# Products of the identity between the first turns, and new orders for the first and last turns of a pipelined kernel

## The reference

```python
down = relu(x @ Wd_b.T + bd); x = x + down @ Wu_b.T + bu          # weights generated per sequence
x = ((layernorm(x) * weight + bias) + tanh(cond)) * weight + bias # layer 1
h = layernorm(x) * g1 + b1; q, k, v = split(h @ W_qkv.T + b_qkv)  # 16 heads of 16
x = x + (softmax(q @ k.T / 4) @ v) @ W_o.T * a1 ...
h = layernorm(x) * g2 + b2; x = x + gelu(h @ W_f1.T + b_f1) @ W_f2.T * a2 ...
val, gate = split(rmsnorm(x) * scale @ up_w.T)
y = act_quant(val * gelu(gate)) @ weight_quant(down_w).T + x
```

## Time and profile before

| | us |
|---|---|
| median of 3 runs | 934.63 (933.69 to 936.41) |
| the profiled execution | 935.74 |
| its span | 933.9 |
| PE busy | 843.1 (90%) |
| DVE busy | 565.4 (61%) |
| ACT busy | 510.9 (55%) |
| POOL busy | 231.2 (25%) |

### The profile page before, as it was taken

The page is one execution under the profiler, slowest core; times in us unless marked ns, Lnnn a source line. Parts: engine busy times, 40 slices in busy tenths (PEclk is TensorE's granted clock), DMA queues, the critical chain, the costliest instruction groups (busy, mean ns, idle before and its releaser), DMA issues.

```text
span 933.9 us, 15916 instructions
## 1 busy us (share of the span) xinstructions
PE 843.1 (90%) x5852; PEld 633.5 (68%) x5852; DVE 565.4 (61%) x1063; ACT 510.9 (55%) x796; POOL 231.2 (25%) x333
## 2 busy tenths in 40 slices
PE   6642577999999999999999999999999999999977
PEld 4101355687777778787878787878777777776665
DVE  1212586575757667575858585858485867656424
ACT  1101444565565657574748575656666574756542
POOL 1001204150405041323232231405050514130310
PEclk9855777999999999999999999999999999999998
DMA  9997643423161433324151515151424132320000
GB/s 344 365 366 252 248 138 124 148 80 122 62 203 38 135 97 114 120 78 156 47 187 47 188 47 188 46 173 61 154 76 142 65 127 80 104 80 25 24 12 12
DMA packets 58477, 118.48 MB, mean 127 GB/s; under 512 B 6336, under 2 KB 15936, under 8 KB 55696
## 3 DMA queue, kind: packets, MB, share of 16 engines
q1 hardware_dynamic: 58400, 117.48, 36.6%
HBM read 82.77 MB, written 34.16 MB: 125 GB/s over the span
## 4 chain that ended last, share of the span: by engine, by line
PE 74%; issue 9%; DMA 7%; DVE 4%; ACT 2%; SPq 2%; POOL 2%; POOLq 0%; DVEq 0%; ACTq 0%
PE bank L486 30%; PE bank L692 11%; PE pair_s L653 6%; PE pair_s L618 5%; PE pair_t L639 5%; PE pair_t L486 4%; DMA hyp<-in_hyper 3%; PE bank L737 3%; PE bank L664 3%; PE bank L567 2%; PE bank L729 1%; PE bank L561 1%; DVE oq L1145 1%; DMA wc<-in_cols 1%; PE bank L574 1%
## 5 line engine op out<-in xcount | busy, mean ns | idle before, releaser
L851 ACT ACTIVATE Pr<-pair_t 128x1024 f32<-128x1024 f32 x128 | 131.3, 1026 | 125.2 <-PE pair_t L639 121.5
L1121 DVE TENSOR_REDUCE nmax<-pair_s 128x4 f32<-128x1024 f32 x128 | 155.8, 1217 | 34.5 <-PE pair_s L618 33.9
L692 PE MATMUL bank<-wf,G 128*128 128x256 f32 x512 | 123.0, 387 | 0.1
L486 PE MATMUL bank<-wup_hi,hD_hi 128*128 128x512 f32 x256 | 109.4, 427 | 4.8 <-POOL hD_lo L1316 4.1
L1344 POOL TENSOR_TENSOR x<-x,xcr 128x512 f32<-128x512 f32 x16 | 20.5, 1281 | 358.1 <-DVE x L1179 358.1
L692 PEld LDWEIGHTS bank<-wf,G 128*128 128x128 f32 x512 | 93.3, 190 | 15.5 <-issue 0.2
L486 PE MATMUL bank<-wup_lo,hD_hi 128*128 128x512 f32 x256 | 102.0, 398 | 0.0
L486 PE MATMUL bank<-wup_hi,hD_lo 128*128 128x512 f32 x256 | 101.9, 398 | 0.0
L618 PE MATMUL pair_s<-Kp,Qp 64*128 64x256 f32 x512 | 66.1, 337 | 21.7 <-DVE nmax L1121 13.0
L895 ACT ACTIVATE gl<-bank,rsD 128x512 f32<-128x512 f32 x64 | 44.1, 689 | 63.6 <-PE bank L486 63.4
L1189 DVE SCALAR_TENSOR_TENSOR hd<-bank,rsD,gl 128x512 f32<-128x512 f32 x64 | 47.9, 748 | 46.2 <-PE bank L486 34.7
(11 more groups left out here) (177 smaller groups left out, 1879.5 us busy)
## 6 DMA issues: line engine op xcount, KB each, us to landing
hyp<-in_hyper SPq DMA_DIRECT2D x16, 1024.0 KB, 10.2
Qp<-qk_scratch SPq DMA_DIRECT2D x64, 256.0 KB, 3.7
Kp<-qk_scratch SPq DMA_DIRECT2D x64, 256.0 KB, 3.6
qk_scratch<-q_hi SPq DMA_DIRECT2D x16, 512.0 KB, 2.8
qk_scratch<-k_hi SPq DMA_DIRECT2D x16, 512.0 KB, 4.0
tC<-rows_scratch SPq DMA_DIRECT2D x16, 384.0 KB, 3.6
cur_scratch<-gen SPq DMA_DIRECT2D x16, 256.0 KB, 10.1
xT_t<-in_xT SPq DMA_DIRECT2D x16, 256.0 KB, 4.2
```

Of the source, the lines that this page charges most:

```text
L486: mm = pe.matmul(dst, l, r, start=first and i == 0, stop=last and i == 2)
L692: mm = pe.matmul(bank[5][:, r * D:(r + 1) * D], G[:, k, r * P:(r + 1) * P], wf2[:, k, :], start=k == 0, stop=k == FT - 1)
L851: act.activation(Pr[:, p % 4, :, :].rearrange("p a n -> p (a n)"), pair_t[:, :, :].rearrange("p a n -> p (a n)"), ACT.Exp, scale=DH ** -0. ...
L1121: dve.tensor_reduce(nmax[:, n % 2, :, p % GP, :], pair_s[:, :, :].rearrange("p a (r n) -> p a r n", r=RT), AX.X, ALU.max, negate=True).the ...
```

## The change

Seven entries W.warm come into PE's table, one in turn 0 between W.qkv and A.q, one between B.o3 of turn 1 and A.up of turn 2, five in turn 2 after B.s0. Each runs keep_clock: three products of the identity by 192 columns into bank 6, whose result nobody reads. In turn 0, ACT's A.down comes ahead of its W.qkv, and DVE's W.qkv comes behind A.cur; ACT splits wf between A.ht and A.q. The tables of turns 0 to 4 are changed for all engines, and in the tail DVE's turn 14 (A.lng and D.u1 swapped) and PE's turn 15 (C.g1 ahead of B.t4, A.v ahead of B.t5). SP waits before each store of q or k that all head loads of the sequence before have landed. The diff, cut:

```diff
     "SP": """
-        0: A.load A.qs A.ks A.ql0 A.kl0 A.ql1 A.ql2 A.ql3 A.kl1 A.kl2 W.late A.kl3 1: B.m0 A.load B.m1 A.qs A.ql0 A.ks A.ql1 2: C.tc 1: A.ql2 A.kl0
-        A.kl1 A.ql3 A.kl2 A.kl3 2: B.m0 A.load B.m1 A.qs A.ql0 A.ql1 A.ql2 A.ks A.kl0 A.ql3 3: C.tc 2: A.kl1 A.kl2 3: A.load B.m0 2: A.kl3 3: B.m1
-        A.qs A.ql0 A.ks A.kl0 D.y0 A.ql1 A.ql2 4: C.tc 3: D.y1 A.ql3 A.kl1 A.kl2 4: B.m0 A.load 3: A.kl3 4: A.qs A.ql0 A.ks A.ql1 B.m1 A.ql2 A.kl0
-        A.kl1 A.ql3 A.kl2 D.y0 D.y1 A.kl3""",
+        0: A.load A.qs A.ks A.ql0 A.ql1 A.kl0 W.late 2: C.tc 0: A.ql2 A.kl1 A.kl2 A.ql3 A.kl3 1: A.load B.m0 B.m1 A.qs A.ql0 A.ql1 A.ks A.ql2 A.kl0
+        A.kl1 A.ql3 A.kl2 A.kl3 2: A.load B.m0 A.qs A.ql0 A.ks B.m1 A.ql1 A.ql2 A.kl0 A.ql3 A.kl1 A.kl2 3: C.tc B.m0 2: A.kl3 3: A.load B.m1 A.qs A.ks
+        A.ql0 D.y0 A.kl0 4: C.tc 3: A.ql1 A.ql2 A.kl1 A.kl2 A.ql3 A.kl3 4: B.m0 A.load 3: D.y1 4: A.qs A.ql0 A.ks A.ql1 A.ql2 A.kl0 A.kl1 B.m1 A.ql3
+        A.kl2 D.y0 A.kl3 D.y1""",
     "PE": """
-        0: A.down A.up W.qkv A.ht A.q A.k A.v 1: A.down A.up B.s0 B.s1 B.s2 B.s3 A.ht B.m0 B.s4 B.s5 B.t0 B.s6 B.t1 B.s7 B.t2 A.q B.m1 A.k B.t3 B.o0
-        B.t4 B.o1 B.t5 A.v B.t6 2: A.down 1: B.t7 B.o2 B.o3 2: A.up C.proj B.s0 B.s1 C.ht B.s2 W.fa W.abs B.s3 C.f0 B.m0 C.f1 B.s4 A.ht C.f2 B.s5 C.f3
...
-        B.o0 4: A.down 3: B.o1 B.t4 C.g0 B.t5 D.y0 D.qt1 B.t6 C.g1 C.g2 B.t7 C.g3 B.o2 B.o3 D.y1 4: B.s0 A.up 3: C.xt 4: C.proj B.s1 D.u0 B.s2 D.u1
-        C.ht B.s3 D.u2 C.f0 C.f1 B.m0 C.f2 B.s4 A.ht C.f3 D.u3 B.s5 A.q B.t0 B.s6 A.k B.s7 D.qt0 A.v B.t1 B.m1 D.y0 B.t2 C.g0 B.t3 C.g1 B.t4 B.o0 B.o1
...
+        0: A.down A.up A.ht W.qkv W.warm A.q A.k A.v 1: A.down A.up B.s0 B.s1 B.s2 B.s3 B.m0 B.s4 A.ht B.s5 B.t0 B.s6 B.t1 B.s7 A.q A.k B.m1 B.t2 B.o0
+        B.t3 B.t4 B.o1 B.t5 A.v B.t6 B.o2 B.t7 2: A.down 1: B.o3 W.warm 2: A.up C.proj B.s0 W.warm B.s1 W.warm W.fa B.s2 W.warm C.ht W.warm W.warm
+        B.s3 C.f0 B.m0 C.f1 B.s4 C.f2 B.s5 A.ht C.f3 B.s6 B.t0 W.abs B.s7 A.q B.m1 B.t1 A.k A.v B.t2 B.o0 C.g0 B.t3 C.g1 B.t4 B.o1 B.t5 C.g2 B.t6 C.g3
+        B.t7 3: A.down 2: B.o2 B.o3 C.xt W.up 3: A.up B.s0 C.proj D.u0 B.s1 D.u1 B.s2 C.ht D.u2 B.s3 C.f0 B.m0 C.f1 B.s4 C.f2 C.f3 A.ht B.s5 B.t0 D.u3
+        B.s6 A.q B.s7 B.t1 A.k B.t2 A.v B.m1 B.t3 B.o0 C.g0 B.t4 B.o1 C.g1 D.qt0 B.t5 C.g2 B.t6 C.g3 B.t7 D.y0 D.qt1 B.o2 B.o3 4: A.down 3: D.y1 4:
+        B.s0 3: C.xt 4: C.proj B.s1 A.up D.u0 B.s2 D.u1 C.ht D.u2 B.s3 C.f0 C.f1 B.m0 C.f2 C.f3 A.ht B.s4 D.u3 B.s5 A.q A.k B.t0 B.s6 A.v C.g0 B.s7
+        B.t1 C.g1 B.t2 B.m1 B.o0 B.t3 C.g2 B.t4 D.qt0 B.o1 B.t5 C.g3 B.t6 D.y0 D.qt1 B.t7 B.o2 D.y1 B.o3 C.xt""",
     "ACT": """
-        0: W.qkv A.down A.lnb A.ht A.q W.fa A.k A.v 1: A.down W.up A.lnb A.ht B.t0 B.t1 A.q B.t2 B.t3 B.t4 A.k B.t5 A.v B.t6 B.t7 2: A.down C.lnb C.ht
-        A.lnb C.f0 C.f1 A.ht C.f2 C.f3 B.t0 A.q B.t1 A.k B.t2 B.t3 B.t4 A.v B.t5 B.t6 B.t7 C.xt 3: A.down D.u0 C.lnb D.u1 C.ht D.u2 C.f0 A.lnb C.f1
...
+        0: A.down W.qkv A.lnb A.ht W.fa A.q A.k A.v 1: A.down A.lnb A.ht B.t0 W.up B.t1 A.q B.t2 B.t3 B.t4 B.t5 A.k B.t6 A.v B.t7 2: A.down C.lnb C.ht
+        C.f0 A.lnb C.f1 C.f2 A.ht C.f3 B.t0 A.q B.t1 A.k B.t2 B.t3 B.t4 B.t5 A.v B.t6 B.t7 3: A.down 2: C.xt 3: D.u0 C.lnb D.u1 C.ht D.u2 A.lnb C.f0
...
     "DVE": """
-        0: W.qkv A.up A.lna A.lng A.ln A.q A.cur A.k 1: A.up A.lna B.s0 A.lng B.s1 A.ln B.s2 B.s3 B.p0 B.m0 B.s4 B.s5 A.cur B.s6 B.s7 B.p1 W.fa B.m1
-        W.up A.q A.k B.o1 W.abs B.o3 2: A.up C.proj C.ln B.s0 B.s1 A.lna A.lng B.s2 A.ln B.s3 B.p0 B.m0 B.s4 B.s5 A.cur B.s6 B.s7 B.p1 A.q A.k B.m1
...
+        0: A.up A.lna A.lng A.ln A.cur W.qkv A.q A.k 1: A.up B.s0 A.lna B.s1 A.lng B.s2 A.ln B.s3 B.p0 B.m0 B.s4 B.s5 B.s6 B.s7 A.cur B.p1 W.fa B.m1
+        A.q W.up B.o1 W.abs A.k B.o3 2: A.up C.proj B.s0 C.ln B.s1 B.s2 A.lna A.lng A.ln B.s3 B.p0 B.m0 B.s4 B.s5 B.s6 B.s7 B.p1 A.q A.cur B.m1 A.k
...
     "PE": """
...
-        D.u1 C.ht B.s3 D.u2 C.f0 B.m0 C.f1 C.f2 B.s4 A.ht C.f3 B.s5 B.t0 D.u3 B.s6 A.q D.qt0 B.s7 B.t1 A.k D.y0 B.m1 B.t2 B.o0 B.t3 C.g0 B.t4 C.g1
-        B.o1 B.t5 A.v B.t6 D.qt1 C.g2 C.g3 B.t7 D.y1 B.o2 B.o3 C.xt 16: B.s0 C.proj B.s1 D.u0 B.s2 D.u1 C.ht B.s3 D.u2 C.f0 C.f1 C.f2 B.m0 C.f3 B.s4
+        D.u1 C.ht B.s3 D.u2 C.f0 B.m0 C.f1 C.f2 B.s4 A.ht C.f3 B.s5 B.t0 D.u3 B.s6 A.q D.qt0 B.s7 B.t1 A.k D.y0 B.m1 B.t2 B.o0 B.t3 C.g0 C.g1 B.t4
+        B.o1 A.v B.t5 B.t6 D.qt1 C.g2 C.g3 B.t7 D.y1 B.o2 B.o3 C.xt 16: B.s0 C.proj B.s1 D.u0 B.s2 D.u1 C.ht B.s3 D.u2 C.f0 C.f1 C.f2 B.m0 C.f3 B.s4
...
                     elif (stage, what) == ("A", "qs"):
+                        if a >= 1:
+                            for j in range(4):
+                                sp.wait_ge(heads_in[j], 32 * a)
...
                     elif (stage, what) == ("A", "ks"):
+                        if a >= 1:
+                            for j in range(4):
+                                sp.wait_ge(heads_in[j], 32 * a)
...
+            def keep_clock():
+                for r in range(3):
+                    pe.matmul(bank[6][:, 0:192], ident, small[:, 0:192], start=True, stop=True)
```

More of the change, by code:

```diff
@@ L79 @@
-        B.t4 B.o1 B.t5 A.v B.t6 2: A.down 1: B.t7 B.o2 B.o3 2: A.up C.proj B.s0 B.s1 C.ht B.s2 W.fa W.abs B.s3 C.f0 B.m0 C.f1 B.s4 A.ht C.f2 B.s5 C.f3
-        B.t0 B.s6 A.q B.s7 B.t1 A.k B.m1 B.t2 B.o0 A.v B.t3 C.g0 B.t4 C.g1 B.t5 B.o1 B.t6 C.g2 B.t7 C.g3 B.o2 B.o3 3: A.down 2: C.xt 3: B.s0 C.proj
-        W.up B.s1 A.up D.u0 B.s2 D.u1 C.ht B.s3 D.u2 C.f0 B.m0 C.f1 C.f2 B.s4 A.ht C.f3 D.u3 B.t0 B.s5 A.q B.s6 A.k B.t1 B.s7 D.qt0 B.t2 A.v B.m1 B.t3
-        B.o0 4: A.down 3: B.o1 B.t4 C.g0 B.t5 D.y0 D.qt1 B.t6 C.g1 C.g2 B.t7 C.g3 B.o2 B.o3 D.y1 4: B.s0 A.up 3: C.xt 4: C.proj B.s1 D.u0 B.s2 D.u1
@@ L83 @@
-        C.ht B.s3 D.u2 C.f0 C.f1 B.m0 C.f2 B.s4 A.ht C.f3 D.u3 B.s5 A.q B.t0 B.s6 A.k B.s7 D.qt0 A.v B.t1 B.m1 D.y0 B.t2 C.g0 B.t3 C.g1 B.t4 B.o0 B.o1
-        D.qt1 B.t5 C.g2 B.t6 C.g3 B.t7 D.y1 B.o2 B.o3 C.xt""",
+        0: A.down A.up A.ht W.qkv W.warm A.q A.k A.v 1: A.down A.up B.s0 B.s1 B.s2 B.s3 B.m0 B.s4 A.ht B.s5 B.t0 B.s6 B.t1 B.s7 A.q A.k B.m1 B.t2 B.o0
+        B.t3 B.t4 B.o1 B.t5 A.v B.t6 B.o2 B.t7 2: A.down 1: B.o3 W.warm 2: A.up C.proj B.s0 W.warm B.s1 W.warm W.fa B.s2 W.warm C.ht W.warm W.warm
@@ L85 @@
+        B.t1 C.g1 B.t2 B.m1 B.o0 B.t3 C.g2 B.t4 D.qt0 B.o1 B.t5 C.g3 B.t6 D.y0 D.qt1 B.t7 B.o2 D.y1 B.o3 C.xt""",
     "ACT": """
-        0: W.qkv A.down A.lnb A.ht A.q W.fa A.k A.v 1: A.down W.up A.lnb A.ht B.t0 B.t1 A.q B.t2 B.t3 B.t4 A.k B.t5 A.v B.t6 B.t7 2: A.down C.lnb C.ht
-        A.lnb C.f0 C.f1 A.ht C.f2 C.f3 B.t0 A.q B.t1 A.k B.t2 B.t3 B.t4 A.v B.t5 B.t6 B.t7 C.xt 3: A.down D.u0 C.lnb D.u1 C.ht D.u2 C.f0 A.lnb C.f1
-        A.ht C.f2 C.f3 D.u3 B.t0 A.q B.t1 B.t2 A.k A.v B.t3 4: A.down 3: D.qt0 B.t4 B.t5 B.t6 B.t7 D.qt1 C.xt 4: D.u0 C.lnb D.u1 C.ht D.u2 A.lnb C.f0
@@ L89 @@
-        C.f1 A.ht C.f2 C.f3 D.u3 A.q B.t0 A.k D.qt0 B.t1 B.t2 B.t3 B.t4 D.qt1 B.t5 A.v B.t6 B.t7 C.xt""",
+        0: A.down W.qkv A.lnb A.ht W.fa A.q A.k A.v 1: A.down A.lnb A.ht B.t0 W.up B.t1 A.q B.t2 B.t3 B.t4 B.t5 A.k B.t6 A.v B.t7 2: A.down C.lnb C.ht
+        C.f0 A.lnb C.f1 C.f2 A.ht C.f3 B.t0 A.q B.t1 A.k B.t2 B.t3 B.t4 B.t5 A.v B.t6 B.t7 3: A.down 2: C.xt 3: D.u0 C.lnb D.u1 C.ht D.u2 A.lnb C.f0
+        C.f1 C.f2 A.ht C.f3 B.t0 A.q B.t1 A.k B.t2 B.t3 D.u3 B.t4 D.qt0 B.t5 A.v B.t6 B.t7 D.qt1 4: A.down 3: C.xt 4: D.u0 C.lnb D.u1 C.ht D.u2 C.f0
@@ L90 @@
+        A.lnb C.f1 C.f2 A.ht C.f3 D.u3 A.q A.k B.t0 B.t1 B.t2 A.v B.t3 B.t4 B.t5 D.qt0 B.t6 D.qt1 B.t7 C.xt""",
     "DVE": """
-        0: W.qkv A.up A.lna A.lng A.ln A.q A.cur A.k 1: A.up A.lna B.s0 A.lng B.s1 A.ln B.s2 B.s3 B.p0 B.m0 B.s4 B.s5 A.cur B.s6 B.s7 B.p1 W.fa B.m1
-        W.up A.q A.k B.o1 W.abs B.o3 2: A.up C.proj C.ln B.s0 B.s1 A.lna A.lng B.s2 A.ln B.s3 B.p0 B.m0 B.s4 B.s5 A.cur B.s6 B.s7 B.p1 A.q A.k B.m1
-        W.tern B.o1 C.g3 B.o3 3: B.s0 C.proj B.s1 C.ln A.up D.u0 B.s2 A.lna A.lng D.u1 A.ln B.s3 B.p0 B.m0 D.quant0 B.s4 D.u2 A.cur B.s5 D.u3 B.s6 A.q
@@ L94 @@
-        B.s7 B.p1 B.m1 A.k D.quant1 B.o1 D.y0 C.g3 B.o3 D.y1 4: B.s0 C.proj B.s1 A.up C.ln D.u0 B.s2 A.lna A.lng D.u1 A.ln B.s3 B.p0 B.m0 D.quant0
-        D.u2 B.s4 B.s5 D.u3 B.s6 A.q B.s7 B.p1 A.k B.m1 D.quant1 A.cur B.o1 D.y0 C.g3 D.y1 B.o3""",
+        0: A.up A.lna A.lng A.ln A.cur W.qkv A.q A.k 1: A.up B.s0 A.lna B.s1 A.lng B.s2 A.ln B.s3 B.p0 B.m0 B.s4 B.s5 B.s6 B.s7 A.cur B.p1 W.fa B.m1
+        A.q W.up B.o1 W.abs A.k B.o3 2: A.up C.proj B.s0 C.ln B.s1 B.s2 A.lna A.lng A.ln B.s3 B.p0 B.m0 B.s4 B.s5 B.s6 B.s7 B.p1 A.q A.cur B.m1 A.k
@@ L96 @@
+        W.tern B.o1 C.g3 B.o3 3: A.up C.proj B.s0 C.ln D.u0 B.s1 A.lna A.lng D.u1 B.s2 A.ln B.s3 B.p0 B.m0 D.quant0 B.s4 D.u2 B.s5 B.s6 A.q B.s7 B.p1
+        A.k B.m1 D.u3 D.quant1 B.o1 D.y0 A.cur C.g3 B.o3 D.y1 4: B.s0 C.proj B.s1 C.ln A.up D.u0 A.lna A.lng D.u1 B.s2 A.ln B.s3 B.p0 B.m0 D.quant0
+        D.u2 B.s4 B.s5 A.cur A.q A.k B.s6 B.s7 B.p1 D.u3 B.m1 D.quant1 B.o1 D.y0 C.g3 D.y1 B.o3""",
     "POOL": """
```

(8 more changed lines are left out.)

## The result

The changed kernel takes 940.0 us (median of 20 runs, 935.36 to 947.33) against 934.5 for the kernel before (20 runs): ratio 1.0062, 95% interval 1.0048 to 1.0076. It is slower by 5.5 us, where 1.9 less was forecast, and outside the range (928.5 to 937.5). Its slowest run (947.33) had a granted clock of 0.901, the other 19 had 0.945 to 0.952. So the two traces differ by 3.6 us only (spans of 937.5 and 933.9).

A forecast was written before the change was run, and what follows sets the result against it. PE's work was taken as the bound in steady turns, leaving gains only at the start, longer-waiting turns and end. Terms -1.2 (through f1 of turn 2), -1.8 (turn 4), +1.05 (turn 15) sum to -1.95: median 932.7 us, range 928.5 to 937.5.

The forecast's parts named there:

- term for cur: Turn 0, DVE: cur lands at 86.2, is combined in 0.68 us, and the wqkv split behind it ends near 88.8.
- Turn 0: Relu starts 3.1 us earlier; A.q starts 1.1 and ends 1.6 earlier, the key store goes out 2.7 earlier.
- Turn 1, weights ahead of heads: SP's weight loads moved ahead of head loads delay kl1: loses 3.9 us, from 2.7 early to 1.2 late.
- Rival 1: Turn 1: head loads are not held by the weights, s2 at 106.9 instead of 110.9; 928.7 us, chance 0.25.
- Turn 1 to 2: Reordered steps up to f0 of turn 2: f0 about 0.8 us late, at 153.9 instead of 153.09.
- The clock: Turn 2: identity products keep the clock up, so f0 and half of f1 take 2.0 us instead of 4.0.
- Rival 2: Turn 2: the clock falls near 147 in spite of the products; 4.8 us worse, 937.5 us, chance 0.15.
- Turn 4 (-1.8): PE's waits of 2.1 us shrink by 1.8: 0.8 for hD_lo, 0.7 for the maxima, 0.3 for keys.
- Rival 3: Turn 4's reordering does not act, since B.m1 behind kl1 on SP is as late as before; 934.5 us, chance 0.20.
- Turn 15 (+1.05): PE's t5 and t6 become adjacent, so t6 waits for t5's exponential, with nothing to hide it: 1.05 us lost.
- The waits of SP (0): SP's added waits for head loads cost 0, as those loads landed 10 us before and SP has time.
- The median: Summed against the profiled 935.74 us, then 1.11 taken off, as the median of three runs was 934.63: 932.7.

The follow-up runs named there:

- mended pair: The mended kernel with the seven groups of identity products and without them: 928.97 us and 932.22 us.
- mended kernel: Changed kernel with weight loads behind ql3, wqkv split ahead of A.cur, B.m1 of turn 4 ahead of kl0, PE's turn 15 as before: 928.97 us, ratio 0.9949.

## Why the prediction was wrong, point by point

Two steps failed. The term for cur in turn 0 made A.q, and with it the key store and the scores, late instead of early; and in turn 4 the wait for the maxima grew instead of shrinking. At proj of turn 5 the forecast was -3.0 and the measurement +3.0. Of these 6.0 us, 2.1 are A.q, 2.1 the key store and the landings behind it; 1.0 was regained up to f0; 2.0 are the waits of turn 4, some 0.6 the orders of turns 2 and 3, which I had put at nothing, and 0.2 stays open. The profiled execution is 5.5 us above its forecast; the median is 7.3 above, since the changed kernel's trace lies 0.7 below its own median and I had taken 1.1 off.

- **Bounds of the kernel:** right. The steady turns are unchanged (491.2 and 491.1 us for ten of them); all differences lie in turns 0 to 4 and 15.
- **Turn 0:** relu and its followers came 3.0 us earlier (3.1 worked out), and the first group took 2.3 as priced. The step that failed is the term for cur: I took it to land at 86.2 and to be combined in 0.68 us; it landed at 87.76 and took 1.32. The 2 MB ahead of it landed at 86.6 instead of 85.6, and cur's second half 1.2 behind them instead of 0.6. The longer combination is a collision with GpSimd that the sum did not have (last section). The split ended at 90.8, not 88.8, and A.q was 1.0 late, not 1.1 early. With the split ahead of A.cur the gain that the edit could have had is there (18.1 us). In four traces with the split behind A.cur and the products in place, A.q began at 18.8 to 20.7: this chain is also an unsteady one.
- **Turn 1, weights ahead of heads:** the mechanism was right, found in kl3's 9.2 us, and it is the largest single loss of the change: forecast 3.9, and 4.2 when undone. As a distance its size was right too: I had s2 8.1 us behind s0 (102.8 and 110.9), and it came 8.03 behind (106.64 and 114.67). Its terms were less so, and that they cancel is luck: from kl0's landing on I had 3.2 for wf2, 2.5 for down_w, 1 for tC and 1.4 for the two heads, and measured were 2.5, 2.5, 1.7 and 1.3. What failed is where s0 starts: +1.5 instead of -2.8 against before, 4.3 us. The key store was to go out 2.7 earlier and went out 0.1 later, counted from the first product (99.03 with the first product at 72.03, against 99.42 and 72.51): 2.8 of the error, and 2.1 of that is A.q, the term of cur again. The rest is landings: 4.14 us for the key store, where before it took 3.50, and 3.4 from kl0's issue (103.24) to s0 instead of the 2.6 that I had taken over.
- **Rival 1** (heads not held): false. In all six traces with the weights ahead of kl1, s2 came 8.0 to 8.7 us behind s0, in the other twelve 4.0 to 4.3; and in after wf2, down_w, tC and kl1 landed in the order of issue (109.1, 111.6, 113.3, 114.6). The prediction read the first of its two sentences from the Trainium skill (DMA: Bandwidth & Descriptors, Queues, rings and completion order) too widely. That page of the Trainium skill says "not FIFO" of a later transfer on one DMA engine beside an earlier one on 16. Its second sentence, that the semaphore's increment lands behind the earlier writes of its DMA engine, agrees with the order of landing here.
- **Turn 1 to 2:** right within 1.0: from s2 to f0 the changed kernel took 42.0 us, before 43.4, forecast 43.0.
- **The clock:** right in the changed kernel: it stayed up, and from f0 of turn 2 to proj of turn 4 the trace is 2.1 us shorter than that of the same orders without products (81.7 and 83.9; forecast 2.0). The mended pair shows 3.3 us by medians, since the first group serves A.q as well. In the orders of before no gain shows in the medians. Rival 2 (the clock falls) did not happen in the changed kernel, but in one of three traces of the kernel before with groups.
- **Turn 4 (-1.8):** this step failed in sign: the waits of turn 4 are 0.2 longer in sum. The 1.1 for hD_lo and the keys came as counted. I saw that SP passes kl0 and kl1 ahead of B.m1 and counted the wait for the maxima 0.7 shorter; it grew by 1.3. kl0 is not a cheap entry: it waits for the landing of a store, 4.6 us after its issue. Measured by undoing it alone: 1.7 to 3.4 us lost. Rival 3 (turn 4 unchanged) was nearer, and also too kind.
- **Turn 15 (+1.05):** right, 1.0.
- **The waits of SP (0):** not settled, 0.2 to 2.3. (They are eight per sequence, four ahead of each store, not seven.)
- **The median:** the sum was made against a trace that was 1.2 us slower than its median of 20 runs, mostly by turn 4 and turn 16. I took its 1.0 us wait for the maxima in turn 4 as something to win. Of eight other traces with the orders of before, one has 0.5 us of this wait and seven have none.

## What to carry to other kernels

On a single transfer queue, moving a large load is moving every load behind it: take from a load that already stands behind it what it adds to a landing (here some 2.5 us per MB), add that to the landing of each load that it passes, and see who waits. An entry that waits for a landing holds what stands behind it on its engine as well, so small, urgent transfers (here the row maxima) go ahead of it. Products without use pay where they fill a gap that exists, ahead of work that would otherwise start at the lower clock (3.3 us in the mended kernel); behind a late weight they are work like any other (0.6 in the changed one).

## What the runs showed of the hardware

- Products of the identity can hold the granted clock. In turn 18 PE idled 2.9 us ahead of D.u0 and its work then ran at 1.2 GHz for 5.3 and 3.4 us (two traces of the kernel before); with two groups in that gap it stayed at 2.4, and proj of turn 17 to the end took 57.7 us (mended kernel) and 58.1 (three traces with the orders of before) instead of 59.1 to 60.3 (fourteen traces).
- The clock falls in turn 16 in some runs and not in others of the same kernel (46.4 and 45.3 us for before, granted clock 0.66 and 1.00 over 852 to 857 us): a single trace can't tell a 1 us gain there.
- VectorE and GpSimd held each other up here. The combination of cur (DVE) took 0.68 us in the kernel before, and 1.32 in the changed one, where GpSimd's hA_lo was under way; it ended 0.55 us behind the end of hA_lo. In the three other traces in which hA_lo began first it took 1.08, 1.24 and 1.75 us and also ended 0.5 to 0.6 behind. In the trace with turn 15 as it was, cur landed earlier and was combined in 0.69 us; there hA_lo took 2.82 us, instead of 1.27, beside the split. In the four traces with the split ahead of A.cur, hA_lo began less than 0.1 us ahead of the end of the combination or later, and they took 0.69 and 1.27 us. Below are the rows of after, then of the kernel with turn 15 as it was:

```profile
87.29 1.27 POOL L1326 TENSOR_TENSOR hA_lo<-hA,hA_hi 128x512 fp32r<-128x512 f32 x1 [4.09 <-ACT hA_hi L840]
87.79 1.32 DVE L1047 SCALAR_TENSOR_TENSOR cur<-cur,base_c 128x512 f32<-128x512 f32 x1 [6.09 <-DMA cur<-cur_scratch]
```

```profile
86.11 0.69 DVE L1047 SCALAR_TENSOR_TENSOR cur<-cur,base_c 128x512 f32<-128x512 f32 x1 [4.93 <-DMA cur<-cur_scratch]
86.72 1.75 DVE L1032 TENSOR_TENSOR wqkv_lo<-wqkv_raw,wqkv_hi 128x1536 fp32r<-128x1536 f32 x1
86.78 2.82 POOL L1326 TENSOR_TENSOR hA_lo<-hA,hA_hi 128x512 fp32r<-128x512 f32 x1 [4.09 <-ACT hA_hi L840]
```
